# Feed-forward block, product stage: magnitudes alone for the last 1,024 rows, with the signed integers rebuilt over their source

## The reference, cut to what matters

```python
def act_qdq(x):
    qmax = 2.0 ** (ACT_BITS - 1) - 1.0
    scale = jnp.maximum(jnp.max(jnp.abs(x)) / qmax, 1e-12)
    return jnp.clip(jnp.round(x / scale), -qmax - 1.0, qmax) * scale
...
x = act_qdq(x)
up = act_qdq(x @ lpbq_dequant(w_up).T)
gate = act_qdq(x @ lpbq_dequant(w_gate).T)
sig = fixed_qdq_u16(jax.nn.sigmoid(gate))
gate = act_qdq(gate * sig)
o = act_qdq(gate * up)
return o @ lpbq_dequant(w_down).T
```

## Time and profile before

| | us |
|---|---|
| median of 3 runs | 1126.76 (1126.33 to 1126.84) |
| the profiled execution | 1126.65 |
| its span in the profile | 1124.9 |
| TensorE busy | 1080.7 (96%) |
| VectorE busy | 996.9 (89%) |
| ScalarE busy | 603.7 (54%) |

### The profile page before, as it was taken

How to read it: one execution, slowest core, us unless ns; L and a number is a source line. 1 busy time by engine, 2 the same in 40 slices (tenths; PEclk the granted TensorE clock), 3 DMA queues, 4 the chain that set the end, 5 groups by cost and what they waited for, 6 DMA issues and landing times.

```text
span 1124.9 us, 20670 instructions
## 1 busy us (share of the span) xinstructions
PE 1080.7 (96%) x8432; PEld 510.7 (45%) x8432; DVE 996.9 (89%) x1394; ACT 603.7 (54%) x707; POOL 45.5 (4%) x57
## 2 busy tenths in 40 slices
PE   8999999999999999999999999999999999999459
PEld 5443344434443444343434344344433443688358
DVE  8787988898999989999989898988799899789996
ACT  3555545555545455555555555545455546457763
POOL 0500000000000000000000000000000002003100
PEclk9999999999999999999999999999999999999769
DMA  8001300010001000101020101010101000000002
GB/s 254 35 20 25 123 21 21 20 39 20 20 21 38 20 20 11 48 1 39 2 58 1 40 1 58 1 39 1 37 14 38 6 30 25 1 1 1 0 1 76
DMA packets 38069, 34.59 MB, mean 31 GB/s; under 512 B 14417, under 2 KB 28946, under 8 KB 37718
## 3 DMA queue, kind: packets, MB, share of 16 engines
q1 hardware_dynamic: 37974, 33.27, 9.6%
HBM read 30.75 MB, written 2.36 MB: 29 GB/s over the span
## 4 chain that ended last, share of the span: by engine, by line
PE 88%; DVE 7%; ACT 2%; issue 2%; DMA 0%; SPq 0%; ACTq 0%; DVEq 0%
PE ps L1576 29%; PE ps L1592 29%; PE ps L1423 5%; PE ps L1518 5%; PE ps L1433 4%; PE ps L1441 4%; PE ps L1818 3%; PE ps L1754 3%; DVE fst L933 2%; PE ps L1452 2%; DVE gt L1313 1%; PE ps L1721 1%; PE ps L1611 1%; PE ps L1412 1%; ACT e_buf L762 1%
## 5 line engine op out<-in xcount | busy, mean ns | idle before, releaser
L762 ACT ACTIVATE e_buf<-ps 128x1024 f32<-128x1024 f32 x400 | 410.7, 1027 | 303.9 <-PE ps L1576 296.3
L1592 PE MATMUL ps<-e_buf,vb 64*64 64x512 f32 x3072 | 400.4, 592 | 0.0
L1059 DVE TENSOR_TENSOR acc<-acc,e_buf 128x1024 f32<-128x1024 f32 x313 | 381.9, 1220 | 0.0
L1156 DVE TENSOR_SCALAR e_buf<-e_buf 128x1024 f32<-128x1024 f32 x400 | 274.1, 685 | 51.5 <-ACT e_buf L762 50.3
L1592 PEld LDWEIGHTS ps<-e_buf,vb 64*64 64x64 f32 x3072 | 113.7, 133 | 211.6 <-issue 197.7
L1576 PE MATMUL ps<-qb,kb_even 64*64 64x512 f32 x1600 | 208.6, 589 | 0.7 <-ACT qb L660 0.7
L1576 PE MATMUL ps<-qb,kb_odd 64*64 64x512 f32 x1600 | 208.8, 589 | 0.0
L1576 PEld LDWEIGHTS ps<-qb,kb_even 64*64 64x64 f32 x1600 | 61.3, 133 | 111.6 <-issue 110.1
L1576 PEld LDWEIGHTS ps<-qb,kb_odd 64*64 64x64 f32 x1600 | 61.3, 133 | 110.4 <-issue 108.5
L1145 DVE TENSOR_TENSOR xacc<-ps,xacc 128x512 f32<-128x512 f32 x54 | 37.2, 691 | 37.6 <-PE ps L1518 37.3
L1754 PE MATMUL ps<-hT,wgu 128*128 128x512 f32 x276 | 64.8, 396 | 0.0
(11 more groups left out here) (196 smaller groups left out, 848.3 us busy)
## 6 DMA issues: line engine op xcount, KB each, us to landing
ebc<-el_rows SPq DMA_DIRECT2D x64, 128.0 KB, 2.9
rden<-inv_rows SPq DMA_DIRECT2D x62, 128.0 KB, 2.9
xacc<-in_x_dram SPq DMA_DIRECT2D x4, 512.0 KB, 9.1
wst<-in_L_xattn_Wkv_dram SPq DMA_DIRECT2D x16, 128.0 KB, 2.6
out_dram<-z SPq DMA_DIRECT2D x7, 256.0 KB, 2.1
wst<-in_L_xattn_Wq_dram SPq DMA_DIRECT2D x8, 128.0 KB, 2.7
wo_raw<-in_L_xattn_Wo_dram SPq DMA_DIRECT2D x8, 128.0 KB, 3.2
acc<-in_ctx_dram SPq DMA_DIRECT2D x2, 512.0 KB, 6.5
```

What stands on the lines that cost most here:

```text
L762: nc.scalar.activation(e_buf[:, g % E_BUFS, :, :], sc[:, g % 2, :, :], ACT.Exp, scale=float(DH) ** -0.5).then_inc(exp_done, 1)
L1059: dve.tensor_tensor(acc[:, t0 % 3, :, :], a, e_buf[:, tiles_to(t0, st) % E_BUFS, :, :], ALU.add).then_inc(summed, 1)
L1156: dve.tensor_scalar(tile, tile, EXP_LO, EXP_HI, ALU.max, ALU.min).then_inc(clip_done, 1)
L1592: ins = pe.matmul(ps_o[DH * h:DH * h + DH, half, :], vb[rows, p % 2, st, DH * h:DH * h + DH], e_buf[rows, g % E_BUFS, h, :], start=(st == ...
```

## The change

- `LATE` goes from 3 to 2: the last two row blocks, 1,024 rows, are done as magnitudes. `SIGNED` goes from 9 to 6, so that 6 of the 12 products are the fused ones.
- `GI_VECTOR` = (0, 2, 4): VectorE converts the gates for n = 2 and 4 too, right ahead of their products, and ScalarE no longer does.
- Twelve signed integer chunks are rebuilt in the output stage instead of six. Those of the gates are written as 16-bit integers over the first half of the f32 gates that they come from (`g_signed` is now a view of `gt`).
- Four groups (4 to 7) instead of two take the multiplication in `out_integers`; groups 4 and 5 wait for six signed chunks, 6 and 7 for twelve.
- `SIGNED_AT` now names three behind cast 1, two behind cast 2, two behind cast 3, three behind cast 4, two behind cast 5.
- `ohl` is laid out as six rows for the feature tiles, with the four parts side by side in each. The wait of `result` for the last `oi_done` is gone.

```diff
--- before.py
+++ after.py
@@ -62,10 +62,11 @@
 FCH = FT * N // FC
 GROUPS = NT // 2
 GI_BUFS = 4
-LATE = NBS - 1
-BY_BLOCK = [e for e in range(FCH) if e % NBS != LATE] + [e for e in range(FCH) if e % NBS == LATE]
-SIGNED = FCH - FCH // NBS
-SIGNED_AT = {2: (0, 1, 2), 3: (3, 4), 4: (5,)}
+LATE = NBS - 2
+BY_BLOCK = [e for e in range(FCH) if e % NBS < LATE] + [e for b in range(LATE, NBS) for e in range(FCH) if e % NBS == b]
+SIGNED = FCH // NBS * LATE
+SIGNED_AT = {1: (0, 1, 2), 2: (3, 4), 3: (5, 6), 4: (7, 8, 9), 5: (10, 11)}
+GI_VECTOR = (0, 2, 4)
 
 
 def rows_of(st):
@@ -335,15 +336,15 @@
                 hT = sb("hT", [P, 2, KT, N], F32R, stack=first)
                 up = sb("up", [P, FT, N], stack=first)
             ui = sb("ui", [P, FT, N], I16, stack=ffn)
-            sb("pad2", [P, (2 * KT * N - FT * N // 2)], stack=ffn)
-            ohl_rows = sb("ohl_rows", [P, 4, N], F32R, stack=ffn)
-            ohl = ohl_rows[:, :, 0:FT * DM].rearrange("p (g i) (f d) -> p g i f d", g=2, f=FT)
             oi = sb("oi", [P, 2, FT, DM], I16, stack=ffn)
+            sb("pad2", [P, (2 * KT * N - FT * N // 2 - FT * DM)], stack=ffn)
+            ohl_rows = sb("ohl_rows", [P, FT, N], F32R, stack=ffn)
+            ohl = ohl_rows[:, :, 0:4 * DM].rearrange("p f (g i d) -> p g i f d", g=2, i=2)
         zf = z[:, :, :].rearrange("p t d -> p (t d)")
         hi16 = zf[:, 0:N].bitcast(I16)
         sg = zf[:, 0:2 * FC].rearrange("p (a f n) -> p a f n", a=2, f=2)
         gi = zf[:, 2 * FC:3 * FC].bitcast(I16).rearrange("p (a f n) -> p a f n", a=2, f=2)
-        g_signed = zf[:, 2 * FC:2 * FC + FT * NB // 2].bitcast(I16).rearrange("p (f n) -> p f n", f=FT)
+        g_signed = [gt[:, :, NB * b:NB * b + NB // 2].bitcast(I16) for b in range(LATE, NBS)]
         su = zf[:, 3 * FC:4 * FC].bitcast(U16T).rearrange("p (a f n) -> p a f n", a=2, f=2)
         wpiece = [zf[:, FF * n:FF * n + FF] for n in range(5)] + [wdown1[:, :]]
 
@@ -855,7 +856,7 @@
             for n, e in enumerate(BY_BLOCK):
                 form = ACT.Copy if n < SIGNED else ACT.Abs
                 nc.scalar.activation(chunk(ui, e), chunk(up, e), form, scale=fsc[:, 2, 2:3]).then_inc(ui_done, 1)
-                if n == 0:
+                if n in GI_VECTOR:
                     continue
                 if n >= GI_BUFS:
                     act.wait_ge(o_done, n + 1 - GI_BUFS)
@@ -863,12 +864,12 @@
 
             def signed_integers(n):
 
-                f = n // 2 * 2
+                late, part = divmod(n, FT)
+                f, e = part // 2 * 2, BY_BLOCK[SIGNED + n // 2]
                 act.wait_ge(o_done, FCH)
-                if n % 2 == 0:
-                    ins = nc.scalar.activation(g_signed[:, f:f + 2, :], chunk(gt, BY_BLOCK[SIGNED + n // 2]), ACT.Copy, scale=fsc[:, 3, 2:3])
+                if part % 2 == 0:
+                    ins = nc.scalar.activation(g_signed[late][:, f:f + 2, :], chunk(gt, e), ACT.Copy, scale=fsc[:, 3, 2:3])
                 else:
-                    e = BY_BLOCK[SIGNED + n // 2]
                     ins = nc.scalar.activation(chunk(ui, e), chunk(up, e), ACT.Copy, scale=fsc[:, 2, 2:3])
                 ins.then_inc(signed_done, 1)
 
@@ -1325,12 +1326,18 @@
             link(ins)
             scale_of(2, 2, pieces, 2)
             link(dve.tensor_tensor(pre[:, 4:5], fsc[:, 3, 1:2], fsc[:, 2, 1:2], ALU.mult))
-            dve.tensor_scalar(gi_at(0), chunk(gt, 0), fsc[:, 3, 2:3], None, ALU.mult).then_inc(gi_first, 1)
+            def product_gates(n):
+
+                if n >= GI_BUFS:
+                    dve.wait_ge(o_done, n + 1 - GI_BUFS)
+                dve.tensor_scalar(gi_at(n), chunk(gt, BY_BLOCK[n]), fsc[:, 3, 2:3], None, ALU.mult).then_inc(gi_first, 1)
+
+            product_gates(0)
             for n, e in enumerate(BY_BLOCK):
-                if n == 0:
-                    dve.wait_ge(gi_first, 1)
+                if n in GI_VECTOR:
+                    dve.wait_ge(gi_first, GI_VECTOR.index(n) + 1)
                 else:
-                    dve.wait_ge(gq_done, n)
+                    dve.wait_ge(gq_done, n + 1 - sum(1 for v in GI_VECTOR if v < n))
                 dve.wait_ge(ui_done, n + 1)
                 if n < SIGNED:
                     dve.tensor_tensor(chunk(gt, e), gi_at(n), chunk(ui, e), ALU.mult).then_inc(o_done, 1)
@@ -1342,6 +1349,8 @@
                     last = BY_BLOCK[n - 1]
                     dve.wait_ge(o_done, n)
                     ins = top(fst[:, 4, 2 * last:2 * last + 2], chunk(gt, last))
+                if n + 1 in GI_VECTOR:
+                    product_gates(n + 1)
             dve.wait_ge(o_done, FCH)
             link(ins)
             scale_of(4, 1, pieces, 3)
@@ -1354,9 +1363,9 @@
                     dve.wait_ge(o_high, g)
                     dve.wait_ge(o_low, g - 1)
                 if DM * g >= NB * LATE:
-                    dve.wait_ge(signed_done, FT)
-                    n0 = DM * g - NB * LATE
-                    dve.scalar_tensor_tensor(out=oi[:, g % 2, :, :], in0=g_signed[:, :, n0:n0 + DM], scalar=fsc[:, 4, 2:3],
+                    late, n0 = g // 2 - LATE, DM * (g % 2)
+                    dve.wait_ge(signed_done, FT * (late + 1))
+                    dve.scalar_tensor_tensor(out=oi[:, g % 2, :, :], in0=g_signed[late][:, :, n0:n0 + DM], scalar=fsc[:, 4, 2:3],
                                              in1=ui[:, :, DM * g:DM * g + DM], op0=ALU.mult, op1=ALU.mult).then_inc(oi_done, 1)
                     return
                 dve.tensor_scalar(oi[:, g % 2, :, r0:r1], gt[:, :, DM * g + r0:DM * g + r1], fsc[:, 4, 2:3], None,
@@ -1371,8 +1380,6 @@
             def result(g):
 
                 dve.wait_ge(f2_ready, g + 1)
-                if g >= GROUPS // 2:
-                    dve.wait_ge(oi_done, GROUPS + 1)
                 dve.scalar_tensor_tensor(out=z[:, 2 * g:2 * g + 2, :], in0=ps[:, g % 4, :].rearrange("p (t d) -> p t d", d=DM),
                                          scalar=fsc[:, 4, 3:4], in1=xacc[:, 2 * g:2 * g + 2, :],
                                          op0=ALU.mult, op1=ALU.add).then_inc(f2_out, 1)
```

## The result

| | median us | lowest to highest | runs |
|---|---|---|---|
| before | 1126.84 | 1126.33 to 1127.32 | 5 |
| changed | 1132.36 | 1131.91 to 1133.85 | 5 |

The ratio is 1.0054, 95% interval 1.0043 to 1.0065: slower, by 5.5 us where 3.3 were forecast. The direction was right, the place too, but the time lies 0.16 us above the range (1128.8 to 1132.2). The profiled execution took 1133.71 us (span 1131.9), one of the two longest of its five.

A forecast was written before the change was run, and what follows sets the result against it. VectorE was taken to bound stage three and TensorE the output stage. From the profiled 1126.65 us, -1.9 for stage three and +5.2 for two stalls gave 1129.95, forecast as a median of 1130.1 us; range 1128.8 to 1132.2.

The forecast's parts named there:

- rival A: Output stage: TensorE's granted clock falls in a stall, adding 1.1 to 2.0 us, 1131.2 to 1132.1 us; chance 0.20.
- The price of a fall: TensorE, output stage: low clock for 3 to 5.4 us, matmuls losing 37% (1.67 of 4.51 us): +1.1 to +2.0 us.
- The page estimate: TensorE's output matmuls at low clock: 213 ns against 117 ns, 45% of the time, +2.4 us for 5.4 us.
- Stage three, -1.9 us: VectorE in the integer product: three maxima fewer, -3.39, two gate conversions more, +1.46; bounds -1.8 and -2.05 us.
- rival C: Stage three: ScalarE becomes the bound or moved conversions wait, so 1.9 us isn't won: 1132.0 us; chance 0.03.
- Two stalls, and their places: Output stage: TensorE waits 2.1 us ahead of group 3 and 3.1 ahead of group 5, through late signed integers 5 and 11.
- The terms put at nothing: Output stage: six-row casts (up to +0.2 us) and integers written over their source (up to +1.0), both taken as 0.
- Their price, 5.2 us: Output stage: total shift of TensorE's groups from the two stalls, 2.1 and 3.1 us.
- overlap of 0.16: TensorE: a matmul takes 280 ns but the next starts after 117, so groups start 0.16 us before the preceding last result.
- B: Output stage: TensorE catches up after the stalls; 3.3 us back, 18 ns a matmul, gives 1126.8 us; chance 0.06.
- D: Output stage: sixth and twelfth signed integers come in time, no stalls, only the -1.9 stands: 1124.9 us; chance 0.02.
- E: Output stage: both stalls, but 0.3 to 0.6 us less each, 1129.0 to 1129.5 us; its lower end has chance 0.05.

The follow-up runs named there:

- the one with a single stall of 3.5 us: Changed kernel with the sixth signed chunk moved from behind cast 3 to behind cast 2: 1130.43 us, ratio 1.0032.
- the kernel with stage three alone: Changed kernel's stage three with the output stage of before; groups 4 and 5 converted from the gates alone, their product left out: 1124.76 us, ratio 0.9982.
- three experiments that touch only the order on one engine: Changed kernel with one signed chunk ahead of cast 3: 1130.43 us; signed-chunk table altered: 1124.98; VectorE's low part ahead of the multiplication in turns 3 and 5: 1127.62.
- with the clock held: Changed kernel with 12 and 20 useless TensorE matmuls ahead of its waits for the low parts of groups 3 and 5: 1130.82 us, ratio 1.0033.

## Why the prediction was off

**The step that failed: the sum had no term for the clock.** It adds two stalls to TensorE at full clock (0.64), although the prediction says that no row shows whether stalls of 2.1 and 3.1 us are enough for a fall. It gave the fall, rival A, 0.20. Both traces of the changed kernel and the one with a single stall of 3.5 us show a fall, the sign that the prediction names for A, and each costs 1.5 us; the two clusters of times fit one or two in each of ten executions. The prediction argued that 2.1 and 3.1 us are shorter than the idle time ahead of the fall in before; one instance of a fall behind a longer pause is no evidence that shorter ones are safe, and with that much unknown the rival deserved far more.

**The price of a fall was wrong in three ways.** It was built for one fall only, with two stalls in the sum. Its length, 3 to 5.4 us, had a row for the 5.4 alone; it was 3.4 each time. Its share, 37%, set the 1.67 us lost against all 4.51 us of the row of warming matmuls, though by the prediction's own reading the clock rose at about 1087.5, 3.4 us after these had begun at 1084.10: 1.67 of 3.4 is 49%. Measured were 1.55 of 3.4 us, 45%. The page estimate beside it, from the Trainium skill, "TensorE: Matmul & The Clock Gate", Part 1, with N / 1.2 GHz from start to start, was 45%, and the trace agrees. That one fall at 1.5 lies within the rival's 1.1 to 2.0 is in part luck: the 2.0 is a length too long times a share too small. The nearness of the 1132.36 to the range's end is luck too: the same kernel's next five executions had a median of 1133.50.

**Stage three, -1.9 us: right.** 1.77 in the trace, 1.9 by the kernel with stage three alone. ScalarE's lead at the end (1.0 forecast, 1.08 measured) and rival C's exclusion held.

**Two stalls, and their places: right.** Idle times of 2.10 and 3.22 against 2.1 and 3.1; three experiments that touch only the order on one engine remove the first, both, or most of both. The terms put at nothing for the casts in six rows and for integers written over their own source were right too: 1.48 and 1.13 to 1.15 us, as before.

**Their price, 5.2 us: too small by 0.6.** The prediction used its 2.1 and 3.1 as gaps and also as the shifts from start to start that it adds up. By its own overlap of 0.16, a gap of 2.10 is a shift of 2.26, so its shift of 2.08 meant a gap of 1.92; the low parts came that much later against TensorE. It also had no term for the new run's first matmul, 0.1 each. The lengths 8.67 and 12.87 show overlap and first matmul together: 0.27 for each run, on top of the idle time.

**The sum as it should have been:** 1126.8 - 1.9 + 5.3 (idle) + 0.5 (cut runs) = 1130.7 unbroken, 1132.3 with one fall, 1133.8 with two. Measured: 1130.8 with the clock held, 1132.36 median, 1133.85 at the top.

**Rivals B, D, E: out.** Runs behind a gap go at 4.20 a group at best, so nothing is caught up; the gaps are there at full length.

## What to carry to other kernels

When a buffer-filling job is spread over an engine's pauses by a table, check each entry against the consumer's deadline: an entry behind an instruction that itself waits for the bottleneck engine comes a full turn late, and whatever is queued behind the consumer's wait goes down with it. A saved stage doesn't pay for that, but here the same work one slot earlier did. And a stall of 2 to 3 us on TensorE has to be priced with its follow-up: the cut run and a stretch at the low clock, once for each stall.

## What the runs showed of the hardware

- The granted clock fell not in the gap but 0.6 to 1.4 us after work had begun again, and the stretch lasted 3.4 us whether the gap had been 2.1, 3.2 or 3.5 us. It cost a run of these matmuls 1.5 us each time (10.22 against 8.67, 14.39 and 14.40 against 12.87).
- Gaps of 0.28 to 0.90 and of 1.32 us brought no fall; one of 2.10 did in one trace and not in the other; those of 3.22 (two traces) and 3.52 did. Work of no use in the gap, leaving 0.44 and 0.51 us idle, kept the clock at 1.00 in the one trace taken (1130.41); that kernel's other four executions took 1131.10 at most.
- A cut in TensorE's run costs more than its idle time: 0.27 us, of which 0.1 is the first matmul behind the gap (384 ns, where the others take 280).
- Writing 16-bit integers over the f32 values that they are made from costs ScalarE 1.13 to 1.15 us for 1,024 elements, as into another tile.
